# Weighted sums of two neighbouring key tiles issued back to back on the matmul engine, in a two-stage attention kernel

## The reference

```python
x = x + tanh(g_xattn[0]) * xattn(layernorm(x), ctx, Wq, Wk, Wv, Wo, bo)
x = x + tanh(g_ffn[0]) * ffn(layernorm(x), ...)

def xattn(x, context, ...):
    sim = einsum('bihd,bjhd->bhij', q, k) * SCALE
    out = einsum('bhij,bjhd->bihd', softmax(sim), v)
    return out @ Wo + bo

def ffn(x, ...):
    q_scaled = (q / norm(q) + query_embedding) * softplus(temperature)
    attn = softmax(einsum('bhqd,bhkd->bhqk', q_scaled, k) / sqrt(hd))
    h = einsum('bhqk,bhkd->bhqd', attn, v)
    # top 3 of 15 routed gates and one shared gate from h, one factor per token
    return (h * masked_gates.sum(-1, keepdims=True)) @ Wp.T + bp
```

## Time and profile before

| | us |
|---|---|
| median of 3 runs | 5065.87 |
| lowest, highest | 5042.02, 5066.6 |
| span of the profiled execution, first to last instruction | 5051.8 |
| PE busy in it | 4766.1 |
| POOL, DVE, ACT busy | 3367.3, 2946.6, 2601.4 |

### The profile page before, as it was taken

How to read it: one execution, slowest core, us unless ns; L and a number is a source line. 1 busy time by engine, 2 the same in 40 slices (tenths; PEclk the granted TensorE clock), 3 DMA queues, 4 the chain that set the end, 5 groups by cost and what they waited for, 6 DMA issues and landing times.

```text
span 5051.8 us, 67410 instructions
## 1 busy us (share of the span) xinstructions
PE 4766.1 (94%) x21696; PEld 2731.3 (54%) x21696; DVE 2946.6 (58%) x4019; ACT 2601.4 (51%) x4705; POOL 3367.3 (67%) x2667
## 2 busy tenths in 40 slices
PE   4999999999999999998998999999999999999997
PEld 3555555556565556564564554554654644645644
DVE  4454545454545454566766656757656666666563
ACT  2444445353535354536636646546556556466454
POOL 1656656574756565747848858767578588578587
PEclk7999999999999999999999999999999999999998
DMA  7343535344343434333233132322323322332320
GB/s 239 97 130 113 129 112 125 117 123 125 97 134 88 142 88 133 93 88 86 57 100 76 45 110 64 84 84 63 94 70 76 93 62 64 92 82 53 101 51 26
DMA packets 285210, 481.11 MB, mean 95 GB/s; under 512 B 32832, under 2 KB 165440, under 8 KB 275648
## 3 DMA queue, kind: packets, MB, share of 16 engines
q1 hardware_dynamic: 284864, 476.79, 34.6%
HBM read 223.14 MB, written 50.33 MB: 54 GB/s over the span
## 4 chain that ended last, share of the span: by engine, by line
PE 50%; DVE 5%; issue 3%; ACT 2%; POOL 1%; SPq 1%; DMA 0%; ACTq 0%; POOLq 0%; DVEq 0%
PE aux L839 15%; PE acc L942 10%; PE aux L902 10%; PE scores L925 9%; DVE nm L1286 4%; PE aux L954 2%; PE aux L963 1%; PE aux L883 1%; POOL added_f L817 1%; PE aux L859 1%; SPq L734 1%; ACT probs L1128 1%; DMA stack<-ck_lo 0%; PE aux L911 0%; DVE st L1223 0%
## 5 line engine op out<-in xcount | busy, mean ns | idle before, releaser
L1286 DVE TENSOR_REDUCE nm<-aux 128x1 f32<-128x1024 f32 x1536 | 1844.7, 1221 | 1192.8 <-PE aux L902 1190.0
L817 POOL TENSOR_TENSOR added<-added,probs 128x512 f32<-128x512 f32 x1433 | 1804.4, 1297 | 856.7 <-PE acc L942 653.4
L1128 ACT ACTIVATE probs<-scores 128x512 f32<-128x512 f32 x2151 | 1189.1, 597 | 862.5 <-PE scores L925 831.3
L925 PE MATMUL scores<-stack 128*128 128x512 f32 x4096 | 1340.3, 417 | 36.3 <-ACT probs L1128 15.8
L902 PE MATMUL aux<-stack 96*128 96x512 f32 (+1 forms) x3072 | 1017.5, 420 | 94.1 <-DVE nm L1286 53.6
L925 PEld LDWEIGHTS scores<-stack 128*128 128x128 f32 x4096 | 735.3, 190 | 639.2 <-ACT probs L1128 223.7
L942 PE MATMUL acc<-probs,vh 128*32 128x512 f32 (+1 forms) x4302 | 968.8, 617 | 20.0 <-ACT vh L1095 20.0
L902 PEld LDWEIGHTS aux<-stack 96*128 96x128 f32 (+1 forms) x3072 | 525.6, 190 | 578.1 <-DVE nm L1286 272.1
L817 POOL TENSOR_TENSOR added_f<-added_f,probs 128x512 f32<-128x512 f32 x537 | 678.9, 1298 | 59.1 <-PE acc L942 36.9
L839 PE MATMUL aux<-xT_hi,wqk 128*128 128x512 f32 x1536 | 580.2, 407 | 13.7 <-ACT qwork L1067 6.9
L1128 ACT ACTIVATE more<-scores 128x512 f32<-128x512 f32 x537 | 300.3, 598 | 155.6 <-PE scores L925 134.7
(11 more groups left out here) (131 smaller groups left out, 4938.1 us busy)
## 6 DMA issues: line engine op xcount, KB each, us to landing
wqk<-w_split SPq DMA_DIRECT2D x256, 256.0 KB, 3.8
wvo<-w_split SPq DMA_DIRECT2D x64, 1024.0 KB, 6.9
stack<-cq_hi SPq DMA_DIRECT2D x128, 256.0 KB, 5.0
stack<-ck_hi SPq DMA_DIRECT2D x128, 256.0 KB, 4.9
stack<-cq_hi SPq DMA_DIRECT2D x256, 128.0 KB, 2.3
stack<-ck_hi SPq DMA_DIRECT2D x256, 128.0 KB, 2.4
xs<-in_x SPq DMA_DIRECT2D x16, 1024.0 KB, 6.4
stack<-cq_lo SPq DMA_DIRECT2D x64, 256.0 KB, 4.9
```

Of the source, the lines that this page charges most:

```text
L817: pool.tensor_tensor(onto, onto, exp_buffer(T, e), ALU.add).then_inc(added_ok, 1)
L925: ins = pe.matmul(scores[:, u % SCORES, :], stack[:, g % 2, e * ph.SLOTS + ks, jt * P:(jt + 1) * P], stack[:, g % 2, e * ph.SLOTS + qs, n ...
L1128: act.activation(exp_buffer(T, e), scores[:, (n - 1) % SCORES, :], ACT.Exp, scale=ph.SCALE).then_inc(probs_ok, 1)
L1286: dve.tensor_reduce(nm[:, e * TT + t:e * TT + t + 1], keys, axis=AX.X, op=ALU.max, negate=True).then_inc(emptied["dve"], 1)
```

## The change

Three edits in the plan; no instruction and no semaphore wait of the emitted code is added or taken away, only the order in each engine's stream differs.

- In `attend`, the item PV of an even step T comes after the last exponential of step T + 1 instead of that of T; the item of an odd step still comes after that of T and after the PV of T - 1.
- Its assumed time is 0.95 instead of 1.05, its due step T + 1.9 for an even T (it was T + 0.9) and -64 for an odd one, so that as soon as it is ready it is taken before all else.
- Both tables `AT` have new values, and `off` moves a number of kinds of items by up to 2.6 steps.

```diff
-AT = (dict(p=[2.5, 18.6, 35.2, 51.9], over=7.4, mx0=3, mxn=3, ctx=[-3.6, 18.6, 24.7, 31.5], load=[5.4, 36.9], norm=[10, 28.5],
-           turned=[20.8, 34.5], out=[63.1, 58.9], xr=43, split=39, off={}),
-      dict(p=[2, 18.6, 36, 50], over=6.5, mx0=0.4, mxn=9, load=[4, 27], norm=[8, 29], turned=[25, 36.6], out=[61, 67], xr=49, off={}))
+AT = (dict(p=[2.57, 19.22, 34.91, 49.37], over=2.91, mx0=3.74, mxn=5.22, ctx=[-3.83, 19.27, 26.82, 28.5], load=[3.67, 43.7], norm=[8.18, 34.95], turned=[21.41, 31.9], out=[63.1, 57.1], xr=41.62, split=51.88, off={"ex": 0.79, "pkl": -0.57, "ssa": -0.17, "ad": 1.02, "mx": -2.11, "mxr": 0.36, "ev": 0.18, "trl": 2.59}),
+      dict(p=[3.43, 18.6, 36.32, 50], over=10.94, mx0=0.34, mxn=8.94, load=[-3.53, 29.75], norm=[4.85, 27.32], turned=[29.76, 33.52], out=[62.06, 61.77], xr=36.35, off={"pkl": -1.62, "pq": -0.35, "pqa": -1.08, "ssa": -0.79, "hs": 0.25, "sma": -0.35, "s2": 0.59, "hsl": -0.43, "tra": 0.4}))
...
-            after = [("ex", T, G - 1), ("PV", T - 1)] + ([("cp", h - 1)] if jt == 0 else [])
+            after = [("ex", T + 1 - jt % 2, G - 1), ("PV", T - 1)] + ([("cp", h - 1)] if jt == 0 else [])
             if T % TURN < TT:
                 after += [("vpe", TT * j + T % TURN)]
-            self.add(("PV", T), "pe", 1.05, T + 0.9, after)
+            self.add(("PV", T), "pe", 0.95, -TURN if jt % 2 else T + 1.9, after)
```

## The result

| | before | after |
|---|---|---|
| median of 4 runs, us | 5066.24 | 5127.76 |
| lowest, highest | 5042.02, 5070.23 | 5123.58, 5134.21 |
| span of the profiled execution | 5051.8 | 5124.5 |
| ratio to before, 95% interval | | 1.0121 [1.0095, 1.0147] |

The change makes the kernel 1.2% slower; the forecast was 3.4% faster. The span grew by 72.7 us.

A forecast was written before the change was run, and what follows sets the result against it. PE, busy 94%, was taken to bound the first stage alone and order the second. Span 5051.8 - 178 - 10 + 15 + 0 = 4878.8 us, plus 14.1 around it, gave 4892 us; range 4815 to 4980.

The forecast's parts named there:

- What bounds the kernel: Whole kernel: PE, busy 94%, alone bounds the first stage and still orders the time in the second.
- Part 1: PVs on PE, both stages: 509 new pairs save 0.35 us each, -178 us.
- Rival A: PVs on PE: only the drain goes, a pair saves 0.24 us, 4948 us; chance 0.11.
- The sign that was named for A or E: Profile after: PE's busy time falling by much less than 170 us would show the forecast wrong.
- E: PVs on PE: pairs don't form, other work due between or values late, about 5066 us; chance 0.03.
- Part 2: First stage, PE's 20.0 us of waits for ACT's copy of the values: between 0 and -20, taken as -10 us.
- Part 3: Second stage: the even PV's delay idles some freed PE time, bounds 0 and 90, taken as +15 us.
- the ring: Second stage's exp buffers: 10, which for four heads make 2.5 tiles; close, but the delay was taken to fit.
- POOL's slack in one half: Second stage: additions take 29.8 of a half's 37.7 us; the 7.9 left fit a delay of about 2.
- Rival D: Second stage: POOL falls behind past its 7.9 us slack, each half grows 5.0 us, 5212 us; chance 0.02.
- Rival B: Second stage gives all its saving back to DVE's maxima and POOL's additions, 90 us idle, 4967 us; chance 0.12.
- Part 4: New steps, both stages: -60 to +60, taken as 0; first stage has nothing to win, -30 at most.

The follow-up runs named there:

- steps_only: The kernel before with only the new step tables, PVs unpaired as before: 5114 us, ratio 1.0101 [1.0064, 1.0137].

## Why the prediction was wrong

**What bounds the kernel** held in part for the first stage, where time taken from PE was to be time taken from the span: some 240 stretches less, 84 us, brought 40 to 43. It failed for the second. "PE still orders the time" there was read from 94% busy; halving DVE's maxima alone, with not one PE instruction less, took 72 us from the seven batches of the kernel before. An engine at 65% was in the way of one at 94%.

**Part 1** was right in its price, 0.35 us a pair (1.86 us after), and in that the pairs form, if not all: 464 stretches less instead of 509. Rival A, that only the drain would go, is out, as one wide matmul is late behind a pair. The sign that was named for A or E came all the same, PE's busy time fell by 58 us and not by 170, for a reason that the text had not thought of: the clock.

**Part 2** was near: 20.0 to 13.7 us.

**Part 3** is the step that failed. It put the cost of holding back the even PV between 0 and the 90 us of PE time that the pairs free there. There is no such upper bound: the hold doesn't only leave freed time unused, it makes engines wait that ran before. The pairs cost 138 us where 78 were to be won in the seven batches, a swing of 216 us, against +15 in the sum. Of the 216, 108 are more idle time of PE and an estimated 51 the lower clock; a term for the clock was missing from the sum. The text had counted the ring (2.5 tiles) and POOL's slack in one half (7.9 us) and asked whether the average fits. It needed to ask who waits at each hold: two tiles of the ring are eight of ten buffers, which by that count leaves ACT two exponentials to run on. Rival D had the kind of mechanism and the sign, with 5.0 us a half; measured are 216 / 56 = 3.9. Its condition was wrong (POOL's late start above a slack of 7.9 us), since without any late first pair 115 of 138 us remain, and so it got a chance of 0.02. Rival B, which let DVE and POOL eat no more than the 90 us, shared Part 3's bound.

**Part 4** took 0 with bounds of -60 to +60 for the new steps. Alone they cost +52 us in the first stage, +12 in the lead, +3 in the seven batches and -4 in the last, 64 us by the spans and 53 by the medians, at the edge of the bounds; the ratio of steps_only is 1.0101 [1.0064, 1.0137]. The bound "nothing to win, so -30 at most" looked at what order can win in a stage that is 98.5% PE, and hardly at what it can lose there: 23 waits for a DMA, and the lower clock behind 17 of them. The second stage's table, in turn, is worth about 100 us together with the pairs, which no sum of separate parts shows.

**The account.** By the spans, before to after: pairs -40 and table +52 make +12 in the first stage, +2 measured; pairs +138 and table +3 make 141 in the seven batches, +46 measured, so that the table takes back some 95; lead and last batch +25.

## What to carry to other kernels

Time freed on the busiest engine is worth its full price at most where every engine that feeds it has room. Before trading a later release for a cheaper order, count at each hold how many buffers the next producers still have, not whether the averages fit: here eight of ten were held, and a saving of 0.35 us a pair turned into a loss. To find what holds, shorten one engine's work at a time in both kernels without touching the order, and read the difference of the two from several runs. Idle time on the matmul engine can cost twice, by itself and by the clock behind it. Where a fixed order is made by a planner, price its new order by stage as a part of its own, and look for waits on DMAs that it takes for landed.

## What the runs showed of the hardware

A PE wait of 3.08 us, in a stage where PE is busy 96% of the time, was followed by 3.4 us at a granted clock of 0.50, in which four matmuls took 1.84 us instead of 0.91. The stage has 22 waits for `ck_lo` of 2.2 to 3.2 us. Behind 17 of them the clock fell to 0.50 in this way; behind 5 it didn't, the longest (3.21 us) among them. A wait of 1.67 us for the same copy in the kernel before had left the clock at 1.00, though one of 1.77 us for the values, at 662 us, hadn't:

```profile
1027.00:1029.80 2.80, 1.13 (x5) 0.63 (x5) 0.00 (x0) 2.80 (x5) 2.80 (x3) 1.00 1.00 234
1029.80:1033.20 3.40, 3.40 (x17) 1.41 (x18) 2.36 (x2) 1.61 (x4) 3.40 (x3) 1.00 1.01 213
```

And the second wide matmul after column groups is late by 0.11 us (it starts 0.34 us behind the first, where 0.23 is usual), besides the first, which starts 0.52 us behind the start of the last record in column groups (medians, before). A pair has this way out once, as the starts of the eight wide ones behind it show.
